# Rounds of eight units on GpSimd, sixteen gather tiles issued row by row, and loops of sixteen units in a graph kernel

## The reference

```
ss, vv = (node_feats @ W_up)[src]                # gather of the sender's row, 128 floats
w = silu(silu(radial(length) @ w0 + b0) @ w1 + b1) @ w2 + b2
mid = products of w, ss, vv and the edge's direction   # 288 floats
msg = segment_sum(mid, dst)                      # scatter-add at the receivers
out = msg @ W_out / 16                           # 128 floats per node
x = layernorm(x + out)                           # every node
```

## Time and profile before

| | before |
|---|---|
| median of the runs | 1247.67 us |
| the profiled execution's own time | 1247.29 us |
| its span, first to last instruction | 1245.5 us |
| busy: PE / DVE / ACT / POOL | 857 / 697 / 534 / 992 us |
| mean granted TensorE clock | 0.846 of full speed |
| rows written by the software queue (GpSimd) | 68,528 packets |

### The profile page before, as it was taken

How to read it: one execution, slowest core, us unless ns; L and a number is a source line. 1 busy time by engine, 2 the same in 40 slices (tenths; PEclk the granted TensorE clock), 3 DMA queues, 4 the chain that set the end, 5 groups by cost and what they waited for, 6 DMA issues and landing times.

```text
span 1245.5 us, 29011 instructions
## 1 busy us (share of the span) xinstructions
PE 857.2 (69%) x6210; PEld 814.8 (65%) x6210; DVE 696.9 (56%) x2916; ACT 534.0 (43%) x1416; POOL 991.8 (80%) x799
## 2 busy tenths in 40 slices
PE   2889777577757775777577757775777577757760
PEld 1789677567656665777567757775776577756760
DVE  6766344456555465376456645655546537645642
ACT  5434332245345444444435525534544444443531
POOL 6778888887888788888888888788878887888885
PEclk9989788878888888788878887888888878887885
DMA  6688884444444544453444454444454445344444
GB/s 171 192 192 178 186 194 75 81 70 100 110 83 71 126 99 70 96 128 71 97 97 78 105 112 70 100 111 83 71 126 99 69 96 128 71 96 96 69 64 90
DMA packets 84582, 131.48 MB, mean 106 GB/s; under 512 B 17150, under 2 KB 68867, under 8 KB 83177
## 3 DMA queue, kind: packets, MB, share of 16 engines
q0 software_dynamic: 68528, 50.71, 31.9%
q1 hardware_dynamic: 15242, 77.95, 18.3%
q10 hardware_dynamic: 687, 1.39, 0.3%
HBM read 78.34 MB, written 77.24 MB: 125 GB/s over the span
## 4 chain that ended last, share of the span: by engine, by line
POOL 40%; DMA 27%; issue 19%; PE 6%; POOLq 3%; SPq 2%; DVE 1%; ACT 1%; ACTq 1%; DVEq 0%
POOL acc L542 24%; DMA acc<-msg,index 21%; POOL sender L513 16%; DMA acc<-in_x_dram 5%; POOLq L519 2%; PE ps_sum L656 2%; PE ps_wts L643 1%; PE ps_msg L668 1%; PE ps_hid L627 1%; SPq L357 0%; DMA sender<-in_x_dram,index 0%; POOLq L541 0%; PE ps_dst L603 0%; POOLq L540 0%; ACT msg L760 0%
## 5 line engine op out<-in xcount | busy, mean ns | idle before, releaser
L542 POOL DMA_INDIRECT acc<-msg,index x391 | 614.2, 1571 | 121.7 <-issue 100.9
L513 POOL DMA_INDIRECT sender<-in_x_dram,index x382 | 374.0, 979 | 120.3 <-issue 102.1
L627 PE MATMUL ps_hid<-hid,mlp 128*128 128x256 f32 x196 | 86.3, 532 | 313.3 <-ACT hid L774 313.3
L1060 DVE TENSOR_TENSOR wts<-ps_wts,bias 128x512 f32<-128x512 f32 x98 | 67.7, 691 | 404.0 <-PE ps_wts L643 401.9
L627 PEld LDWEIGHTS ps_hid<-hid,mlp 128*128 128x128 f32 x196 | 38.7, 247 | 321.5 <-ACT hid L774 321.5
L656 PEld LDWEIGHTS ps_sum<-same,mid 128*128 128x128 f32 x1568 | 238.3, 224 | 11.5 <-DVE mid L1075 0.8
L656 PE MATMUL ps_sum<-same,mid 128*128 128x128 f32 x1568 | 245.0, 308 | 0.7 <-DVE mid L1075 0.7
L759 ACT COPY msg<-ps_msg 128x128 f32 (+1 forms) x98 | 26.0, 265 | 409.5 <-DMA acc<-msg,index 365.5
L668 PE MATMUL ps_msg<-outw,sumT 128*128 128x64 f32 x1568 | 186.0, 272 | 0.0
L668 PEld LDWEIGHTS ps_msg<-outw,sumT 128*128 128x128 f32 x1568 | 182.8, 192 | 0.0
L748 ACT COPY sumT<-ps_sum 128x512 f32<-128x512 f32 x196 | 114.6, 584 | 144.3 <-PE ps_sum L656 141.4
(11 more groups left out here) (144 smaller groups left out, 1030.7 us busy)
## 6 DMA issues: line engine op xcount, KB each, us to landing
acc<-in_x_dram SPq DMA_DIRECT2D x80, 312.5 KB
total<-acc SPq DMA_DIRECT2D x30, 832.0 KB
out_dram<-normed SPq DMA_DIRECT2D x29, 832.0 KB
by_row<-in_x_dram SPq DMA_DIRECT2D x1152, 0.5 KB
acc<-msg,index POOLq DMA_INDIRECT x391, 3.3
sender<-in_x_dram,index POOLq DMA_INDIRECT x382, 3.4
out_dram<-normed ACTq DMA_DIRECT2D x1, 832.0 KB
vec_raw<-in_edge_attr_dram SPq DMA_DIRECT2D x1, 576.0 KB
```

Of the source, the lines that this page charges most:

```text
L513: pool.indirect_dma_start(sender[:, u % SRING, i, :], None, x, bass.IndirectOffsetOnAxis(ap=index[:, u, 0, i:i + 1], axis=0)).then_inc(fet ...
L542: pool.indirect_dma_start(acc, bass.IndirectOffsetOnAxis(ap=index[:, v, 1, i:i + 1], axis=0), msg[:, v % RING, i, :], None, compute_op=ALU.add
L627: pe.matmul(ps_hid[:, 2:4, :], mlp1[:, :], hid0[:, k % 2, :], start=True, stop=True).then_inc(hid1_ps, 1)
```

## The change

- `BATCH` 2 to 8: GpSimd issues the gathers of eight units, then the scatters of eight. The gathers run `AHEAD` = 12 units ahead at the start of the loop and, within a round, four units beyond the round's first. The sender ring grows to 16 units and the message ring to 8. To make room, the raw edge arrays lie in `total` and `normed`, which the dense part uses later.
- Sixteen tiles come by single rows: slot 3 of units 17, 25, ... 97 (eleven) from SyncE, and slot 2 of units 27, 43, 59, 75, 91 (five) from ScalarE. SyncE issues the rows of units 17 and 25 between the pieces of the copy, eight rows after each two pieces; the others in two groups of 16 per pair as before. ScalarE issues its rows in thirteen groups of 12 or 8, one per unit, between `turned` and `msg_out`. The sender numbers of the looped tiles are loaded a second time, into two small tables.
- TensorE, ScalarE and SyncE run units 12 to 91 in a loop of five bodies of 16 units. TensorE's waits then compare with a register.
- `src_first` is loaded alone: SyncE issues its last row, and both queues wait until it has landed before they load anything else.

```diff
-LAG = 8
-RING = 4
-SRING = 10
-BACK = 2
-BATCH = 2
+AHEAD = 12
+RING = 8
+SRING = 16
+BATCH = 8
-BY_ROW = tuple(range(27, UNITS, 8))
-ROWS_AT = (16, 16, 16, 16, 16, 16, 16, 16)
+IN_LOOP = 12
+BODY = 16
+BODIES = (UNITS - IN_LOOP) // BODY
+LAST = IN_LOOP + BODY * BODIES
+SP_UNITS = tuple(range(IN_LOOP + 5, UNITS, BODY // 2))
+SP_ROWS = 16
+ACT_UNITS = tuple(range(IN_LOOP + BODY - 1, LAST, BODY))
+ACT_ROWS = (12, 8, 12, 8, 12, 8, 12, 8, 12, 8, 12, 8, 8)
...
+        def single_rows(engine, kind, u, i, ids, a, n):
+            _, ids = nc.values_load_multi_w_load_instructions(
+                ids[:, a:a + n], engines=(kind,),
+                min_val=0, max_val=N - 1, skip_runtime_bounds_check_because="src names rows of x")
+            for p in range(n):
+                engine.dma_start(by_row[a + p:a + p + 1, row_slot(u, i), :], x[bass.ds(ids[p], 1), :]
+                                 ).then_inc(row_in[row_slot(u, i)], 16)
...
         def _(sp):
+            rows, values = flat(src_first, src, 1)
+            load_last(sp, rows[FIRST - 1:FIRST, :], values, 1, first_in, pad=True)
+            sp.wait_ge(first_in, 16 * 3)
             load_main(sp, dst_raw, dst, 1, edges_in)
...
-            with sp.Fori(PIECES_FIRST // 2, PIECES // 2) as h:
+            sp.wait_ge(src_in, 16)
+            for h in range(PIECES_FIRST // 2, PIECES // 2):
                 for b in range(2):
                     copy(h, b)
+                if 2 <= h < 2 + 2 * SP_ROWS:
+                    u = SP_UNITS[(h - 2) // SP_ROWS]
+                    single_rows(sp, mybir.EngineType.SP, u, G - 1, ids_of(u, G - 1),
+                                (h - 2) % SP_ROWS * (P // SP_ROWS), P // SP_ROWS)
+                if h == SP_ROWS:
+                    load_ids()
...
+            def rows_of(first, j, step):
+                if step == 0:
+                    sp.wait_ge(senderT_ps, first + BODY * j - BODY + 1)
+                    sp.sem_inc(sp_passed, 1)
...
+            with sp.Fori(0, BODIES - 1) as j:
+                for m in range(BODY // 2):
+                    first = SP_UNITS[2 + m // half_body]
+                    pair(IN_LOOP // 2 + BODY // 2 * j + m, (first, j, 2 * (m % half_body)))
...
-            for u in range(LAG):
+            for u in range(FIRST):
                 gathers(u)
             pool.wait_ge(index_in, 1)
+            for u in range(FIRST, AHEAD):
+                gathers(u)
...
             for v in range(0, UNITS, BATCH):
-                orders = [order_of(u) for u in range(v, v + BATCH)]
-                for u in range(v + LAG, min(v + LAG + BATCH, UNITS)):
-                    gathers(u)
-                for u in range(v, v + BATCH):
+                orders = []
+                for u in range(v, min(v + BATCH, UNITS)):
+                    if 0 < v and u + AHEAD - BATCH < UNITS:
+                        gathers(u + AHEAD - BATCH)
+                    orders.append(order_of(u))
+                for u in range(v, min(v + BATCH, UNITS)):
                     scatters(u, orders[u - v])
...
-            for u in range(UNITS):
+            for u in range(IN_LOOP):
+                unit(u, u)
+            with pe.Fori(0, BODIES) as j:
+                for k in range(IN_LOOP, IN_LOOP + BODY):
+                    unit(BODY * j + k, k, j=j)
+            for u in range(LAST, UNITS):
                 unit(u, u, following=u < UNITS - 1)
...
                     turned(u + 1, k + 1, stage_next=not isinstance(u, int) or u + 3 < UNITS)
+                if body is not None and k - IN_LOOP < len(ACT_ROWS):
+                    rows_of(body, k - IN_LOOP)
                 if k >= 1:
                     msg_out(u - 1, k - 1)
...
-            load_last(act, rows[FIRST - 1:FIRST, :], values, 1, first_in, pad=True)
+            act.wait_ge(first_in, 16 * 3)
```

More of the change, by code:

```diff
@@ L234, in bass_gnn @@
         gathered = [[sem(f"gathered{b}_{i}") for i in range(G)] for b in range(2)]
-        row_in = [sem(f"row_in{b}") for b in range(ROW_SLOTS)]
+        row_in = [sem(f"row_in{b}") for b in range(3)]
         basis_staged = sem("basis_staged")
@@ L327, in slots_done, with row_slot @@
             return slot_done[v % 2][i], 16 * (v // 2 + 2 - missing)
+        LANES = ((SP_UNITS, G - 1, (0, 1)), (ACT_UNITS, G - 2, (2,)))
+        def row_slot(u, i):
+            for units, slot, buffers in LANES:
+                if i == slot and u in units:
+                    return buffers[units.index(u) % len(buffers)]
         def fetched(u, i):
@@ L443, in pair @@
                             store(h, b)
-                some_rows(2 * j)
+                if rows is not None:
+                    rows_of(*rows)
                 for h, b, now in orders_of(j + NORM_AFTER):
@@ L448, in pair @@
                         load(h, b)
-                some_rows(2 * j + 1)
-            for j in range(PAIRS):
-                pair(j)
+                if rows is not None:
+                    rows_of(rows[0], rows[1], rows[2] + 1)
+            half_body = P // SP_ROWS // 2
+            sp.wait_ge(ids_in, 16 * len(ID_LISTS))
+            for j in range(IN_LOOP // 2):
+                pair(j)
+            with sp.Fori(0, BODIES - 1) as j:
+                for m in range(BODY // 2):
+                    first = SP_UNITS[2 + m // half_body]
+                    pair(IN_LOOP // 2 + BODY // 2 * j + m, (first, j, 2 * (m % half_body)))
+            for j in range(LAST // 2 - BODY // 2, PAIRS):
+                m = j - (LAST // 2 - BODY // 2)
+                pair(j, (SP_UNITS[-1], 0, 2 * m) if m < half_body else None)
             done = sp.value_load(done_count[0:1, 0:1], min_val=0, max_val=CHUNKS)
@@ L591, in _, with turn @@
             pe.wait_ge(loaded, 16 * WEIGHT_DMAS)
[L593 removed]
+            def turn(u, k, j=None):
                 b = k % 2
@@ L611, in turn @@
                         pe.wait_ge(*fetched(u, i))
[L612 to L614 removed]
+                    arrived = sender[:, k % SRING, i, :]
+                    if row_slot(k, i) is not None:
+                        arrived = by_row[:, row_slot(k, i), :]
                     mm = pe.transpose(ps_sT[:, P * i:P * (i + 1)], arrived, ident[:, :])
@@ L775, in silu0, with unit @@
                                bias=bias0[:, :]).then_inc(hid0_ready, 1)
-            def unit(u, k, tail=False, meanwhile=None):
+            def unit(u, k, tail=False, meanwhile=None, body=None):
                 b = k % 2
@@ L831, in dense @@
                                 normalise(order // 4, b, part)
-                    unit(2 * j + part, k + part, meanwhile=dense)
+                    unit(2 * j + part, k + part, meanwhile=dense, body=body)
             stage(0, 0)
@@ L837, in _ @@
             turned(0, 0)
-            first = RING // 2 + 2
-            for u in range(2 * first):
+            for u in range(IN_LOOP):
                 unit(u, u)
             act.wait_ge(tables, 1)
-            with act.Fori(first, PAIRS - 2) as j:
-                pair(j, 2 * first)
-            for j in range(PAIRS - 2, PAIRS):
+            act.wait_ge(ids_in, 16 * len(ID_LISTS))
+            with act.Fori(0, BODIES) as j:
+                for m in range(BODY // 2):
+                    pair(IN_LOOP // 2 + BODY // 2 * j + m, IN_LOOP + 2 * m, j)
+            for j in range(LAST // 2, PAIRS):
                 pair(j, 2 * j)
```

122 lines of the change are left out of this document (66 added, 56 removed).

## The result

The changed kernel takes 1233.43 us (median of 4 runs, 1231.30 to 1235.05), the kernel before 1247.43 beside it (1246.41 to 1247.75). The ratio is 0.9888, 95% interval 0.9871 to 0.9905: 14.0 us faster, where 17.4 were forecast. It lies in the forecast's own range of 1224 to 1237. Its profiled execution took 1235.05 us (span 1233.0), at a mean granted clock of 0.845 (before 0.846).

What follows compares the result with a forecast made beforehand. POOL's list of gathers and scatters was taken as the bound: 1247.3 - 8.75 - 8 - 2.3 + 1 = 1229.3, with 0.4 and half a microsecond for the crowded start 1230 us. Own range 1224 to 1237, with rivals 1223 to 1254.

Steps and rivals of the forecast that it cites:

- What bounds it: POOL's list of 382 gathers and 391 scatters is the time; everything that shortens it shows one for one.
- Fewer gathers: POOL: 375 gathers, 7 fewer, at 1.25 us each, -8.75 us.
- Fewer switches: POOL: 33 fewer rounds with both gathers and scatters, some 0.25 us each, -8.3 us, taken as -8.
- Rival C: POOL: the switch isn't what costs and the start gains nothing, 1238 us; chance 0.10.
- `src_first` alone: Kernel start: first indices land earlier, so the first gather comes earlier, -2.3 us, bounds 0 and -3.5.
- Rows in the copy: SyncE's copy: row groups end it near 235 us instead of 189, delaying chunk load and moments; +1 us, bounds 0 and +20.
- Covered almost exactly: +1: Units 19 to 23 after the late moments: message 23 ready at 320 us, due at 319, costing +1 us.
- rival B: Copy: it ends late and stalls POOL once, first chunk load at 275 instead of 256, 1242 us; chance 0.08.
- Rows on ScalarE: ScalarE's sequencer: rows make units 10 to 12 us, under the 12.2 us a unit that POOL needs; the compute fits.
- Rival A: ScalarE's sequencer between `turned` and `msg_out`: compute becomes the bound, deciding from 12.5 us a unit, 1262 us; chance 0.18.
- The price of the low clock: TensorE, paused by ScalarE's rows: 1.2 GHz costs 1.85 us a unit; all row units slow give 10.9, with waits 11.7.
- The end: Kernel's end: stays as before, with the same 10.6 us behind the last scatter.

Runs made afterwards that it cites:

- c4: The kernel before with only `src_first` loaded alone: 1244.40 us, 0.9976 of the kernel before.
- d4: The changed kernel with the dense part two pairs later and ScalarE's five tiles gathered by GpSimd (380 gathers): 1235.12 us, 0.9900 of the kernel before.
- c2: The changed kernel with the dense part starting two pairs later (`DENSE_FROM` 4 to 6): 1228.84 us, 0.9859 of the kernel before.
- c3: The changed kernel with rounds of two units instead of eight: 1235.69 us, 0.9904 of the kernel before.
- c1: The changed kernel itself, measured again beside its variants: 1233.64 us, 0.9886 of the kernel before.
- d3: The changed kernel with scatters of 16 of 128 rows and ScalarE's five tiles gathered by GpSimd: 1155.47 us, 0.9263 of the kernel before.
- d1: The changed kernel with each scatter adding only the first 16 of 128 rows: 1154.17 us, 0.9252 of the kernel before.

## Why the prediction was right, step by step

*What bounds it.* POOL's list, read from the earlier trace rows, is the time. The shortenings showed nearly one for one, until a message was late: `c4` gave 3.05 of 3.7 us, `d4` against `c2` the price of five gathers within the noise. Right.

*Fewer gathers.* -8.7, as forecast.

*Fewer switches.* Forecast -8.3 and taken as -8, with 0.25 us each. The first two DMAs of every run give -8.0, and `c3` against `c1` measures 0.22 each. Rival C (the excess belongs to something else) is refuted by that pair. So the term was right. What failed is that it was the only change of POOL's durations in the sum: the scatters inside the runs grew by 3.2 us, for which the forecast had no term, and so the third row of the table shows -5.6. `c3`, with rounds of two, has this growth too (4.1 us over the kernel before), `d4`, without ScalarE's rows, 4.9, and `c4` only 0.4. So neither the long rounds nor ScalarE's rows nor `src_first` makes it. Left are SyncE's added rows, the larger rings and the loops, and which of these it is stays open.

*`src_first` alone.* First gather at 5.16, forecast 6.6: -3.7 instead of -2.3, just past the bound of -3.5. Of the 5.2 us from issue to cast in the earlier trace rows, 3.7 went when the others were held back and the small parts had a queue of their own; `c4` has both and doesn't split them.

*Rows in the copy.* The forecast had turns of 5.7 to 5.9 us (5.5 measured), the copy's end at 235 (229.8), the load at 256 (248.49), the moments at 265 (253.11), message 23 ready at 320 and due at 319. Up to the moments all came earlier, by up to 12 us; the message came later, at 322.25. The price was +5.5 and not +1. The step that failed is "Covered almost exactly: +1": it added up only VectorE's delay and 10.5 us a unit. Message 19 was ready at 273.67, 4 us before its forecast, but from there to message 23 it took 48.6 us instead of 42. Of these, 4.84 are ScalarE's normalisation waiting for the store at 310.61, which SyncE had behind its row groups; the rest is units of about 11 us. The message was due at 317.8 and came 4.45 us late. Without the wait for the store it would have been ready near 317.4, in time (an estimate from these rows). It is rival B's outcome, a late copy that stalls POOL once, at less than half of its price, but not by rival B's way: the first load stood at 248.49, and not at 275. In a step whose cover is one microsecond, each queue that the late work passes had to be followed one step further. `c2`, `c3` and `d3` bear this out: the wait for the store is in all three, it costs POOL nothing where it falls into gathers (`c2`) or has more gathers ahead of the message (`c3`), and it grows when ScalarE's rows are taken away (`d3`, 13.16 us against 6.47 in `d1`). No run removes the wait itself. The two tiles that the copy carries save 2.5 us of gathers, less than the 5.5 that the stall costs; only with the dense part later (`c2`) do they pay.

*Rows on ScalarE.* Forecast 10.5 us from `silu0` to `silu0` with 12 rows and 8.9 with 8. Measured are 11.1 us in most of both (above, 273.50 to 284.63 with 8 rows and on to 295.72 with 12; with 8 rows 9.1 to 9.6 at the shortest), and 7 to 8 without; the shortest distance at each place of the loop is 10.2 in the mean, so the 8-row figure was too low and the forecast's 10 to 12 held. In the unit with 12 rows they begin beside the engine's normalisation, at 289.94; in the one with 8 they begin only at 280.38, behind its last copy, and that is how 8 rows come to take as long. Ahead of the message copy the engine stands 3.7 us there with nothing to do. Rival A would have needed 12.5; after 330 us POOL waits for ScalarE's message no longer than 0.3 us in the changed kernel, and its only idle time above 0.34 is one of 0.85, put down to a scatter's landing. In `d1` the compute feeds a POOL that needs 11.1 us a unit, so the point from which it would decide lies no higher. The price of the low clock did not show in the sum: from 331 to 1200 us the granted clock is 0.86 of full speed and was 0.85 before. It moved within a round, to 0.69 in the gathers from 528 us and 0.91 in the scatters behind them (the windows view), and just ahead of the gathers TensorE had been idle (its timeline):

```profile
528.00:566.00 38.00, 28.10 (x166) 25.87 (x166) 14.21 (x63) 13.27 (x36) 28.63 (x31) 0.69 0.36 100
566.00:626.00 60.00, 44.78 (x327) 41.91 (x325) 35.79 (x150) 30.71 (x81) 50.16 (x33) 0.91 0.52 82
...
530.99 0.47 PE L682 MATMUL ps_sT<-ident,sender 128*128 128x128 f32 x1 [12.65 <-DMA sender<-in_x_dram,index]
```

The Trainium skill ("TensorE: Matmul & The Clock Gate", part 1), by which the slow clock is the default and activity lifts it, agrees with the trace. TensorE had stood 12.65 us for a gather of the new round, since the gathers run only four units ahead at a round's end; in the 14 us from 528 the granted clock is 0.50, the level of 1.2 GHz, and from 566, with TensorE at work again, 0.91.

*The end.* 10.60 and 10.64 us behind the last scatter: right.

The forecast of 1230 stands against 1233.4 with two errors of one sign (stall 4.5 more; POOL's other DMAs 2.2 longer, +3.2 and -1.0) and two of the other (first gather 1.4 better, crowded start 0.6), and with the profiled execution's place among its runs. That the errors partly cancel is luck: with the start as forecast the time would have been near 1235 (an estimate).

## What to carry to other kernels

When one engine's list is the time, every item taken off it counts in full, and a switch between kinds of work on it can be measured by one pair of kernels that differ in the length of the rounds. Sort such an engine's durations by their place in a round before you call a term wrong: here a right term and a missing one stood in one sum. What pays for the items moved is the list they are moved to: follow that list past the first wait that it delays, through the stores and loads queued behind, to the next consumer on the critical engine. Whether a late item costs anything depends on what that engine has in its list at that moment. Longer rounds also mean that due times come closer together within a round, so a cover that held on average must be checked at the round's last message.

## What the runs showed of the hardware

- An indirect scatter-add of 16 rows of 128 floats occupied GpSimd for 1.29 us, one of 128 rows for 1.57, each with 0.30 ahead. 112 rows more cost 0.28 us, so most of it is a price per instruction.
- Going from gathers to scatters and back cost 0.22 us in GpSimd's durations per round.
- ScalarE's queue issued 12 rows of a register's address in 4.8 us (289.94 to 294.77 in the changed kernel), the first of them beside the engine's own work; then the engine stood 3.8 us until the message copy. Five tiles this way showed no cost in time (`d4` against `c2`), since POOL's list is longer than ScalarE's.
- On one chip the kernels that ran elsewhere too took 22 to 30% longer, and hundreds of small sequencer steps, most of them SyncE's, took 0.7 us instead of under 0.1.
